# Other order of the experts' loads, fills and stores in a macaron block with a mixture of experts, on one Trainium2 core

## The reference, cut to what matters

```python
def ffn(x, ...):                       # x: 8192 tokens of 128
    logits = silu(x @ rw1 + rb1) @ rw2 + rb2          # 8 experts
    w = softmax over the two largest logits of a token, 0 elsewhere
    h = silu(einsum('nd,edh->enh', x, we1) + be1)     # 128 -> 512
    eo = einsum('enh,ehd->end', h, we2) + be2         # 512 -> 128
    return x + einsum('ne,end->nd', w, eo)
x = x + 0.5 * ffn(layernorm(x))
x = x + linear_attention_block(layernorm(x))          # 32 sequences of 256, 16 heads, then gelu MLP
x = x + 0.5 * ffn(layernorm(x))                       # same weights again
```

## Time and profile before

| | us |
|---|---|
| median of 3 runs | 2080.32 (2077.67 to 2083.05) |
| the profiled execution | 2079.63 |
| its span | 2077.1 |
| f1, up to the last in-transpose of expert tile 38 | 476.1 |
| attention, between the barriers | 505 to 1704, about |
| f2 and the output | 1704 to 2077.1 |

### The profile page before, as it was taken

The page is one execution under the profiler, slowest core; times in us unless marked ns, Lnnn a source line. Parts: engine busy times, 40 slices in busy tenths (PEclk is TensorE's granted clock), DMA queues, the critical chain, the costliest instruction groups (busy, mean ns, idle before and its releaser), DMA issues. The chain is left out here.

```text
span 2077.1 us, 36379 instructions
## 1 busy us (share of the span) xinstructions
PE 1711.5 (82%) x12527; PEld 1385.3 (67%) x12527; DVE 1559.4 (75%) x4230; ACT 1074.7 (52%) x1935; POOL 935.1 (45%) x973
## 2 busy tenths in 40 slices
PE   3357688894799999999999999999999847899980
PEld 2236466673687877777777777777777735677770
DVE  6667576664778889888888889898888636677763
ACT  2235456563456565555555564555555414566660
POOL 5756400002653545565455546545552323455551
PEclk9998899997899999999999999999999967999995
DMA  6554465662000000010010001001100004666648
GB/s 222 166 182 157 169 228 194 208 236 72 11 12 7 11 17 11 17 20 15 13 19 17 12 17 22 17 9 19 19 13 8 12 11 180 231 233 222 218 163 255
DMA packets 99151, 190.30 MB, mean 92 GB/s; under 512 B 15021, under 2 KB 61786, under 8 KB 87962
## 3 DMA queue, kind: packets, MB, share of 16 engines
q1 hardware_dynamic: 53402, 141.48, 19.8%
q0 software_dynamic: 31616, 35.95, 7.2%
q10 hardware_dynamic: 13952, 10.55, 1.6%
HBM read 131.08 MB, written 56.85 MB: 90 GB/s over the span
## 5 line engine op out<-in xcount | busy, mean ns | idle before, releaser
L1557 POOL TENSOR_TENSOR at_sc<-at_sc 128x512 f32<-128x512 f32 x128 | 198.2, 1548 | 344.2 <-DVE at_sc L1675 344.0
L1972 POOL DMA_INDIRECT x<-finished_rows,slot x128 | 207.6, 1622 | 295.4 <-DMA finished_rows<-f_rows_out 259.8
L567 ACT ACTIVATE f_hid<-f_up_ps,f_w 128x512 f32<-128x512 f32 x312 | 214.6, 688 | 191.5 <-PE f_up_ps L442 164.2
L1667 DVE SCALAR_TENSOR_TENSOR at_qk<-at_exps,at_relus 128x512 f32<-128x512 f32 x256 | 183.0, 716 | 101.2 <-ACT at_relus L1466 98.7
L1675 DVE TENSOR_TENSOR at_sc<-at_s_ps,at_mask 128x384 f32<-128x384 f32 x512 | 251.5, 548 | 1.1 <-PE at_s_ps L1290 1.1
L898 DVE TENSOR_TENSOR f_hid_lo<-f_hid,f_hid_hi 128x512 fp32r<-128x512 f32 x312 | 208.9, 687 | 14.7 <-ACT f_hid_hi L574 1.9
L671 POOL DMA_INDIRECT expert_rows<-f_rows_out,f_dest x156 | 155.5, 997 | 129.7 <-DVE f_rows_out L921 93.4
L1530 ACT ACTIVATE raw<-at_num_ps 128x512 f32<-128x512 f32 x128 | 76.2, 595 | 241.2 <-PE at_num_ps L1327 220.4
L660 POOL DMA_INDIRECT sent_rows<-f_xn,slot x144 | 146.3, 1016 | 74.6 <-issue 40.3
L1287 PE MATMUL at_s_ps<-at_qk 64*128 64x256 f32 x1024 | 171.0, 411 | 6.5 <-issue 5.6
L1465 ACT ACTIVATE at_exps<-at_proj_ps 128x512 f32<-128x512 f32 x253 | 152.4, 603 | 37.1 <-PE at_proj_ps L1265 30.3
(11 more groups left out here) (322 smaller groups left out, 4767.3 us busy)
## 6 DMA issues: line engine op xcount, KB each, us to landing
f_w<-split_weights SPq DMA_DIRECT2D x78, 1028.0 KB, 4.9
f_got<-sent_rows SPq DMA_DIRECT2D x78, 264.0 KB, 4.4
finished_rows<-f_rows_out SPq DMA_DIRECT2D x39, 256.0 KB
split_weights<-f_split SPq DMA_DIRECT2D x8, 1024.0 KB
sent_rows<-f_pads SPq DMA_DIRECT2D x16, 264.0 KB
x<-in_L_attn_x SPq DMA_DIRECT2D x16, 256.0 KB, 5.1
raw<-in_L_ffn_we SPq DMA_DIRECT2D x16, 256.0 KB
out_x<-x ACTq DMA_DIRECT2D x16, 256.0 KB, 4.5
```

The costliest lines, as they stand in the source:

```text
L567: A(hid[:, c, :], up_bank(n)[:, :], ACT.Silu, bias=w[:, i % RING_W, 4 * HID + c:4 * HID + c + 1].bitcast(FP32)).then_inc(s_silu, 1)
L1557: g.tensor_tensor(sc[:, n % RING_SC, :, 3, :], sc[:, n % RING_SC, :, 1, :], sc[:, n % RING_SC, :, 2, :], ALU.add).then_inc(s_sum, 1)
L1667: stt(full, exps[:, p % 2, :], 1.0, relus[:, p % 2, :], ALU.min, ALU.add).then_inc(s_phi, 1)
L1972: nc.gpsimd.indirect_dma_start(out=k.x[:, first:first + D], out_offset=None, in_=k.done[:, :], in_offset=bass.IndirectOffsetOnAxis(k.slot[ ...
```

## The change: what it does

The settings: `EARLY` goes from 9 to 11; f1 has `begin` 9 and `join` 11 (before 8 and 10), so 6 expert tiles run beside routing there; f2 has `join` 15, so 2 do. `back_at` is 4i + 9 everywhere. On the SP queue two weights and two rows come first, and then weights and rows in turn; the fills stand behind tile 8's loads in f1 and behind tile 4's in f2 (before: behind tile 8's in both, with `EARLY` 9). Tile 11 is the first whose rows wait for the fills and for all sends (before: tile 9). The stores of f1 are issued by POOL: the first five in the routing loop, and the other 34 behind it. The fill value's memsets move behind 1/std on POOL. The constants of the attention except `head_sel_f` are made by POOL behind f1's fifth store. The first two sequences of the attention are gathered without add, into two unused ends of x, and DVE adds them. In f2 the tables are made ahead of the first normalisation. In the attention, POOL sends both halves of the last routed tile one step earlier, ahead of a 1/std. The numbering of tokens changes, so that a `load_back` reads one run of 2 KB for each partition rather than two of 1 KB.

```diff
-EARLY = 9
+EARLY = 11
...
-                engine.dma_start(taken(t, j).rearrange("p (s n) -> p s n", s=2), back_rows(t, j)).then_inc(s_taken[t], 16)
+                engine.dma_start(taken(t, j), k.back[j * TOKENS + t * TILE:j * TOKENS + (t + 1) * TILE, :]
+                                 .rearrange("(p q) d -> p (q d)", q=TQ)).then_inc(s_taken[t], 16)
...
-            return HC * i + 9 if HC * i + 9 < ALONE else HC * i + 11
+            return HC * i + 9
...
             sp.wait_ge(s_table, 2)
-            for i in range(RING_W):
-                load_weights(i)
+            load_weights(0)
+            load_weights(1)
             for i in range(RING_XN):
                 if sent_by(i, begin):
                     sp.wait_ge(s_sent[i], sent_by(i, begin))
-            for i in range(RING_IN):
-                load_rows(i)
-            for i in range(RING_W, EARLY):
+            load_rows(0)
+            load_rows(1)
+            for i in range(2, EARLY):
                 load_weights(i)
                 load_rows(i)
-                if out is None:
-                    store_rows(i - RING_IN)
-            sp.wait_ge(s_pads, n_pads)
-            sp.wait_ge(s_ends, 1)
-            for e in range(E):
-                pad_end(e)
+                if i == with_rows + 2:
+                    sp.wait_ge(s_pads, n_pads)
+                    sp.wait_ge(s_ends, 1)
+                    for e in range(E):
+                        pad_end(e)
...
             for i in range(EARLY + 1, NTILES):
                 load_weights(i)
                 load_rows(i)
-                if out is None:
-                    store_rows(i - RING_IN)
...
         # POOL, ffn_phase
-                g.memset(k.x[:, 0:TILE], 0.0)
-                g.memset(k.x[:, (k.tiles + 1) * TILE:(k.tiles + 2) * TILE], 0.0)
+            inverse_std(start)
+            inverse_std(start + 1)
+            if start + 2 < T:
+                inverse_std(start + 2)
             if not loads:
                 g.memset(pads[:, :, :, 0:D], 0.0).then_inc(s_pads, 1)
...
-            inverse_std(start)
-            inverse_std(start + 1)
-            if start + 2 < T:
-                inverse_std(start + 2)
...
+                if out is None and t >= join:
+                    store_rows(t - join)
+            if loads:
+                k.make_attention_constants(nc, pool, zeroed)
             if out is None:
+                for i in range(with_rows - 1, NTILES):
+                    store_rows(i)
                 for i in range(RING_OUT):
                     pool.wait_ge(s_back[i], back_count(i))
                 pool.wait_ge(s_moved, 2 * 2 * E + 1)
-                k.gather_back(0, 0)
+                k.gather_first(0)
...
         # DVE, ffn_phase
+            if begin == start:
+                dve.wait_ge(s_so_far, 1)
+                early_tiles()
             normalise(start)
...
-            if begin == start:
-                early_tiles()
             x_lo(start)
...
         # POOL, attention_phase
-            add_back(1, 0)
-            add_back(0, 1)
-            add_back(1, 1)
             inverse_std("A", 1)
+            k.gather_first(1)
             inverse_std("B", 1)
             inverse_std("A", 2)
...
-                    if u >= 2 and placed_in(s) is not None:
+                    if u >= 2 and placed_in(s) is not None and s < NB:
                         send(placed_in(s), u - 2)
+                    if u == 1 and placed_in(s) is not None and s >= NB:
+                        send(placed_in(s), 0)
+                        send(placed_in(s), 1)
...
         # DVE, attention_phase
-            dve.wait_ge(s_added[0], 64)
+            def add_first(i):
+
+                dve.wait_ge(s_added[i], 64)
+                for j in range(2):
+                    first = i * (k.tiles + 1) * TILE + j * BT
+                    if j:
+                        dve.wait_ge(s_first, 2 * i + 1)
+                    tt(k.x[:, xc(i)], k.x[:, xc(i)], k.x[:, first:first + BT], ALU.add).then_inc(s_first, 1)
+                dve.wait_ge(s_first, 2 * i + 2)
+
+            add_first(0)
...
+        def gather_first(i):
+
+            for j in range(2):
+                for q in range(BT // P):
+                    first = i * (k.tiles + 1) * TILE + j * BT + q * D
+                    nc.gpsimd.indirect_dma_start(out=k.x[:, first:first + D], out_offset=None, in_=k.done[:, :],
+                                                 in_offset=bass.IndirectOffsetOnAxis(k.slot[:, i * (BT // P) + q, j:j + 1], 0),
+                                                 ).then_inc(k.added[i % 4], 16)
...
-        ffn_phase(nc, k, "f2", start=k.routed, begin=k.routed, join=k.tiles, out=tile_out)
+        ffn_phase(nc, k, "f2", start=k.routed, begin=k.routed, join=k.tiles - 1, out=tile_out)
```

More of the change, by code:

```diff
@@ L354, in _ @@
                     sp.dma_start(dst, src).then_inc(later_in, 16)
-            if out is None:
-                for i in range(NTILES - RING_IN, NTILES):
-                    store_rows(i)
             for i in range(RING_OUT):
@@ L1602, in _ @@
                                     pattern=[[-1, UNITS], [-32, 2], [0, DH]], channel_multiplier=1).then_inc(s_const, 1)
-            g.affine_select(out=low_rows_4[:, :], in_=low_rows_4[:, :], compare_op=ALU.is_ge, fill=0.0, base=31,
-                            pattern=[[32, 4]], channel_multiplier=-1).then_inc(s_const, 1)
             add_back(2, 0)
@@ L1775, in _ @@
             first_mean("B", 0, y_of(0))
-            dve.wait_ge(s_added[1], 64)
+            low(1)
+            normalise("B", 1, lambda q: z[:, q, :], y_of(0), s_z)
+            low(2)
+            hT_low(0)
+            add_first(1)
             first_mean("A", 1, x_of(1))
-            normalise("B", 1, lambda q: z[:, q, :], y_of(0), s_z)
-            low(1)
-            hT_low(0)
             normalise("A", 2, y_of(1), x_of(1), s_y)
-            low(2)
             dve.wait_ge(s_y, 2)
@@ L1974, in gather_back, with make_attention_constants @@
                                              compute_op=ALU.add).then_inc(k.added[i % 4], 16)
-        k.gather_back = gather_back
+        def gather_first(i):
[5 more added lines that the diff above has]
+                                                 ).then_inc(k.added[i % 4], 16)
+        def make_attention_constants(nc, pool, done):
+            g = nc.gpsimd
+            g.memset(k.mask[:, :, :], 1.0).then_inc(done, 1)
+            g.memset(k.den_sel[:, :, :], 0.0).then_inc(done, 1)
+            g.memset(k.low_rows_4[:, :], -1.0).then_inc(done, 1)
+            pool.wait_ge(done, k.n_zeroed + 3)
+            for blk in (0, 2):
+                g.affine_select(out=k.mask[:, blk, :], in_=k.mask[:, blk, :], compare_op=ALU.is_ge, fill=0.0, base=0,
+                                pattern=[[1, P]], channel_multiplier=-1).then_inc(done, 1)
+            g.affine_select(out=k.low_rows_4[:, :], in_=k.low_rows_4[:, :], compare_op=ALU.is_ge, fill=0.0, base=-16,
+                            pattern=[[-32, 4]], channel_multiplier=1).then_inc(done, 1)
+            g.affine_select(out=k.den_sel[:, :, :], in_=k.den_sel[:, :, :], compare_op=ALU.not_equal, fill=1.0,
+                            base=0, pattern=[[1, 4], [-1, 32]], channel_multiplier=0).then_inc(done, 1)
+            pool.wait_ge(done, k.n_zeroed + 7)
+            g.affine_select(out=k.den_sel[:, :, :], in_=k.den_sel[:, :, :], compare_op=ALU.not_equal, fill=1.0,
+                            base=16, pattern=[[1, 4], [-1, 32]], channel_multiplier=0).then_inc(done, 1)
+            g.affine_select(out=k.low_rows_4[:, :], in_=k.low_rows_4[:, :], compare_op=ALU.is_ge, fill=0.0, base=31,
+                            pattern=[[32, 4]], channel_multiplier=-1).then_inc(done, 1)
+        k.gather_back, k.gather_first, k.make_attention_constants = gather_back, gather_first, make_attention_constants
         k.we1, k.we2 = we1, we2
```

44 lines of the change are left out of this document (14 added, 30 removed).

## The result

On the first chip the changed kernel takes 2012.1 us (median of 4 runs, 2005.34 to 2018.92) against 2078.99 for the kernel before: ratio 0.9675, 95% interval 0.9647 to 0.9704. The forecast was 2016 us, with a range of 1996 to 2052. The profiled execution after is the quickest of the four, 2005.34 us with a span of 2003.6; against 2079.63 (span 2077.1) that is 73.5 us of span, 6.6 more than the medians differ (66.9).

A forecast was written before the change was run, and what follows sets the result against it. Expert stages were taken as bound by TensorE's program and its waits, not a busy share. Terms -6 - 9 - 24 - 1 - 2 - 6.5 - 10 - 5.4 = -64 from the profiled 2079.6 gave 2016 us, range 1996 to 2052.

The forecast's parts named there:

- Terms 1 and 2: f1 up to tile 11: fewer expert tiles beside routing, -6 us; hole at the fills partly filled by tile 7, -9.
- Routing itself ends where it did: f1's start: with one expert tile fewer beside routing, routing's end does not move; part of the -6 us.
- tile 9's rows still stand behind the fills in SP's queue, so this stays: f1, tiles 8 to 11: the 22.7 us from first fill to tile 9's rows remain; part of the -9 us.
- Term 3: f1's 27 tiles alone: stores leave SP's queue, so rows load about 1.9 us earlier; -24 us (-15 to -31).
- Terms 4 and 5: f1 to attention: DVE's wait for first rows goes, -1 us; attention's end: last sends ahead of a 1/std, -2.
- Term 6: f2's start: memset off the norm, tables hidden ahead of it, fills beside earlier tiles; -6.5 us (-2 to -10).
- the fills, now behind tile 4, run beside tiles 1 to 4: f2's start: fills run beside tiles 1 to 4 rather than before tile 9; -2 us.
- Terms 7 and 8: f2's 27 tiles alone: out-transpose waits go, -10 us; tail: scatters released earlier, loads back in 2 KB runs, -5.4.
- A: Both expert stages: rows' time from issue to landing sets 7.085 us a tile; 2034 us in all, chance 0.25.
- B: Routing: stores on POOL hold the sends, up to 1.5 us in each of five iterations; near 2036 us, chance 0.11.
- C: Both expert stages: PE waits for nothing, 6.5 us a tile; 2000 us in all, chance 0.07.
- D: f1 alone: POOL's stores delay the rows' landing, from 9.35 us a tile; 2081 us at 9.4, chance 0.03.

The follow-up runs named there:

- a_join: Changed kernel with `EARLY` 9 and f1's `begin` 8 and `join` 10 as before, fills behind tile 8 in f1; 1961.67 us, ratio 0.9635.
- a_stores_late: Changed kernel with f1's stores back on SP, the store of tile i-5 behind the loads of tile i; 1938.52 us, ratio 0.9543.
- b_back9: Kernel before with the gate product at 4i + 9 everywhere as the only change, stores still on SP; 2021.87 us, ratio 0.9751.
- a_back11: Changed kernel with the gate product of the stage alone back at 4i + 11, stores on POOL; 1986.33 us, ratio 0.9784.
- b_stores_pool: Kernel before with f1's stores issued by POOL as the only part of the change; 2059.43 us, ratio 0.9922.
- before_again: The kernel before, unedited, run once more on chip 8 as reference; 2074.72 us.
- a_stores_sp: Changed kernel with f1's stores back on SP, the store of tile i-4 behind the loads of tile i; 1953.85 us, ratio 0.9609.

## Why the prediction was right, step by step

**Terms 1 and 2 (-15, measured -13.8): right in sum, wrong in its parts.** Two steps failed. The first is "Routing itself ends where it did". The last send ends 11.4 us earlier. POOL's rows before, the wait ahead of the tenth routing tile's sends and the last send:

```profile
147.53 1.04 POOL L643 TENSOR_TENSOR f_rstd<-f_var_eps,minus_half 128x4 f32<-128x4 f32 x1 [14.75 <-DVE f_var_eps L696]
237.32 1.34 POOL L660 DMA_INDIRECT sent_rows<-f_xn,slot  x1 [0.30 <-issue]
```

Now:

```profile
134.67 1.04 POOL L625 TENSOR_TENSOR f_rstd<-f_var_eps,minus_half 128x4 f32<-128x4 f32 x1 [2.24 <-DVE f_var_eps L690]
226.27 1.00 POOL L648 DMA_INDIRECT sent_rows<-f_xn,slot  x1 [0.30 <-issue]
```

Before, PE stood 12.75 us for tile 0's rows with the next routing tile behind it; now it reaches tile 0 at 139.15 and waits for nothing there (4.1 us on chip 8, where it had been 11.2). The counts follow, and with them the first fill: 213.64 instead of 224.94. The second failed step is "tile 9's rows still stand behind the fills in SP's queue, so this stays", with a hole near 9 us left before tile 9. They stand there, but nothing is waited for from tile 8 on, and tiles 8 to 11 take 21.3 us. PE's longest wait near routing's end is 7.49 us ahead of an up matmul, just before tile 8 (16.4 us from tile 7 to 8). The kernel before had the same 7.49 us, 11.4 us later; the profile ties it to nothing. What has gone is the 7.46 us before tile 9. Tiles 0 to 8 take 3.4 more. a_join shows what the forecast left out: what must be hidden is not only the fills but the wait of tile `EARLY`'s rows for the last sends.

**Term 3 (-24, measured -37.0 and, on chip 8, -31.2): the mechanism holds, the size was short.** Rows go out 0.21 us behind the output copy (median), as forecast. I took 6.75 us a tile and left 6 us of waits at the `later` loads. Measured: 6.50 and 1 to 5 us. The 6.75 leaned on the 6.8 that I got by taking the waits out of 212.5 us. That left in what the waits did to the clock: the stretches right behind the three longest waits (3.42, 2.56 and 3.70 us, at tiles 16, 20 and 28) had a granted clock of 0.79, 0.79 and 0.70, and took 8.06, 8.09 and 8.97 us with no wait in them. The division was off too. I gave the gain to the store and gave the gate product a number in f2 alone. Alone, the store brings 18.5 us and the product 25.8; together 31.2, so they overlap: behind the early product the store's move is left 5.4 us, behind the store's move the product 12.7 (single profiled runs on chip 8, the changed kernel's the slowest of its four). The store on SP costs when it waits, because the product is late; without the wait (a_stores_late) SP is as good a place as POOL. That POOL's stores would stall beside DVE's copies, which I weighed, did not show: they took 0.54 to 0.78 us on POOL, and the stage with them is as quick as the one without (176.3 and 176.1 us).

**Terms 4 and 5 (-3, measured -1.2).** DVE's wait of 9.14 us is gone; it waits 15.54 us at the barrier instead (9.95 before) and 4.41 for B's 1/std (up to 7 forecast). From tile 38 to the first norm it takes 34.3 instead of 38.7 us, and this is given back behind it: the score matmuls that started at 547.3 us, 32.5 behind the first norm, start at 498.1, 38.5 behind it. From there to the last scores the attention's body has kept its time (1100.5 and 1100.0 us), and from the last scores to f2's first norm it takes 52.8 instead of 55.0.

**Term 6 (-6.5, measured -2.0 with the hole).** The half before tile 0 is right: 18.2 us from 25.2, and `f_var_eps` takes 0.17 us where the earlier trace rows had 2.43. The wrong step is "the fills, now behind tile 4, run beside tiles 1 to 4": on this chip they last 22.3 us, PE is busy for 13.1 of them with the tiles that were loaded, up to tile 4, and tile 5's weights and rows stand behind them. The term gave the fills no length; on the quick chips they take 8.4 us and there is no hole. Why they take longer beside POOL's sends on this kind of chip is not shown.

**Terms 7 and 8 (-10 and -5.4, measured -11.9 and -7.6): right.** b_back9 alone gives 13.1 us in f2 and 5.3 up to the last scatter; a_back11 takes them away. The last scatter ends 25.0 us after tile 38 instead of 30.2, and from there to the end it is 37.8 instead of 40.3 us. This goes with the 2 KB runs: the four kernels traced with 1 KB runs, b_back9 among them, take 40.3 to 40.8 us there, the ten with 2 KB 37.8 to 38.8.

**The rivals.** A (the landing of rows sets 7.085) falls: f2 runs at 6.64. B (POOL beside routing) doesn't show: an iteration takes 13.5 to 13.6 us instead of 13.46, a store being 0.6 us of it. C, 6.5 us a tile in both stages, came true in f1 only. D never came near.

## What to carry to other kernels

When one stage runs slower than its twin, look for what stands in the in-order queue between its loads and for which late producer it waits; then move the producer ahead before moving the queue, since here that one line brought more than a second engine's queue. A wait in a queue can cost through what is queued behind it, even where the next load itself isn't held: the 2.3 us of a store pushed a bulk load into the next tile's transfers. Ask of a fixed piece of work which tile is the first that needs it, not only where it is issued. And where two kinds of work share an engine in a fixed order, as routing and expert tiles do here on PE, a wait of the one holds the other: the 12.75 us before tile 0 had put off all later sends.

## What the runs showed that I had not expected

- Gathers without add are shorter on POOL than gathers that add: seven of the eight take 0.94 to 1.06 us, one 1.83, against 1.54, for the same 128 rows of 512 bytes.
- With f1's 39 stores on POOL's queue its way through the next barrier is longer: 9.07 us from the last gather to POOL's next operation, 5.22 without them. The difference is in the DRAIN at the barrier, in fourteen traces of fourteen, also when the stores alone are moved (b_stores_pool: 9.99 us, before_again: 7.22). What it waits for is open.
- Chips differ in kind: the same kernel takes 2074 to 2079 or 2032 to 2034 us. The stages with experts alone don't differ; the attention (1192.5 or 1169.7 us in the changed kernel, with a granted clock of 1.00 from 600 to 1500 us in both), the routing stretch (granted clock 0.85 to 0.92 or 1.00, from 150 to 195 us) and eight fills beside POOL's sends (22.3 and 21.0 us, or 8.4) do, and the change is worth 0.9644 to 0.9675 on one and 0.9565 on the other.
- A wait of 2.4 to 3.9 us on PE costs more than itself: 5 us of slower matmuls beside 9.2 us of waits in a_stores_sp.
